# Graph network kernel: filler matmuls placed anew at three places, and one source one-hot per short tile made by ScalarE

## The reference, cut to what matters

```python
msg = x[src] @ W_msg.T + b_msg + edge_embed[type]
messages = segment_sum(msg, dst)                       # one row per node
r, z = sigmoid(...), sigmoid(...)                      # GRU gates from messages and x
n = tanh(i_n + r * h_n)
x1 = layernorm(x + (1 - z) * n + z * x)
h = relu(x1 @ w_self1 + mean_agg(x1, src, dst) @ w_neigh1 + b1)
y = h @ w_self2 + mean_agg(h, src, dst) @ w_neigh2 + b2
out = layernorm(x1 + y)
```

## Time and profile before

| | |
|---|---|
| median of 3 runs | 734.29 us (732.76 to 736.21) |
| the profiled execution | 735.67 us; its span from first to last instruction 733.9 us |
| mean clock granted to TensorE | 0.971 of full |
| TensorE busy | 648.3 us, 88% of the span |
| VectorE busy | 466.9 us, 64% |
| ScalarE busy | 242.2 us, 33% |
| GpSimd busy | 165.0 us, 22% |

### The profile page before, as it was taken

How to read it: one execution, slowest core, us unless ns; L and a number is a source line. 1 busy time by engine, 2 the same in 40 slices (tenths; PEclk the granted TensorE clock), 3 DMA queues, 4 the chain that set the end, 5 groups by cost and what they waited for, 6 DMA issues and landing times.

```text
span 733.9 us, 14577 instructions
## 1 busy us (share of the span) xinstructions
PE 648.3 (88%) x3061; PEld 308.6 (42%) x3061; DVE 466.9 (64%) x1469; ACT 242.2 (33%) x486; POOL 165.0 (22%) x348
## 2 busy tenths in 40 slices
PE   1668889999999999898967999789999999999995
PEld 0222333443433444343323444334555546666663
DVE  6879999999999999999992366641010001144334
ACT  3034553442332255566763245531121122100000
POOL 2432233333223333343430012130111011100000
PEclk9969999999999999999996999989999999999998
DMA  5000000000000000000011011010111011212200
GB/s 161 1 1 0 1 1 0 1 1 1 1 0 1 1 1 1 0 1 1 1 35 51 15 36 51 17 46 15 44 43 43 1 43 41 82 44 61 62 25 16
DMA packets 29441, 17.38 MB, mean 24 GB/s; under 512 B 1841, under 2 KB 28223, under 8 KB 29400
## 3 DMA queue, kind: packets, MB, share of 16 engines
q1 hardware_dynamic: 29400, 16.82, 7.8%
HBM read 10.38 MB, written 6.44 MB: 23 GB/s over the span
## 4 chain that ended last, share of the span: by engine, by line
PE 59%; DVE 22%; issue 9%; DVEq 6%; ACT 2%; POOL 0%; ACTq 0%; POOLq 0%
DVE S L624 12%; PE PS L1267 11%; PE PS L923 11%; PE PS L996 9%; PE PS L880 5%; DVE D L618 4%; PE PS L1178 3%; PE PS L1057 3%; PE PS L1105 2%; DVEq L624 2%; PE PS L1231 2%; PE PS L1094 2%; PE PS L1166 2%; PE PS L1167 1%; PE PS L1030 1%
## 5 line engine op out<-in xcount | busy, mean ns | idle before, releaser
L624 DVE TENSOR_SCALAR S<-iota_h,src_col,src_w 128x440 bf16<-128x440 f16 x749 | 253.2, 399 | 0.2 <-issue 0.2
L923 PE MATMUL PS<-S,D 128*128 128x449 bf16 x780 | 213.1, 363 | 36.8 <-DVE S L624 32.9
L477 POOL COPY S<-T 128x27 bf16 (+1 forms) x262 | 107.6, 412 | 222.2 <-PE PS L923 210.0
L923 PEld LDWEIGHTS PS<-S,D 128*128 128x128 bf16 x780 | 75.3, 97 | 169.2 <-DVE S L624 127.7
L1310 ACT ACTIVATE AT<-digits 128x1152 uint8 (+5 forms) x75 | 77.2, 1031 | 148.6 <-DVE digits L613 148.6
L618 DVE TENSOR_TENSOR D<-iota_t,dst 128x384 bf16<-128x384 f16 x260 | 93.5, 360 | 13.9 <-PE PS L923 13.2
L880 PE MATMUL PS<-AT,xp 128*128 128x512 bf16 x375 | 100.6, 379 | 0.0
L1267 PE MATMUL PS<-xp,AT 128*128 128x384 bf16 (+1 forms) x525 | 85.6, 326 | 0.0
L996 PE MATMUL PS<-AT,x1p 128*128 (+2 forms) x375 | 68.8, 342 | 1.2 <-DVE slot L806 1.2
L1267 PEld LDWEIGHTS PS<-xp,AT 128*128 (+2 forms) x525 | 51.5, 98 | 33.9 <-issue 0.3
L923 PE MATMUL PS<-S,AT 128*128 128x449 bf16 x150 | 35.9, 378 | 19.2 <-DVE S L624 10.5
(11 more groups left out here) (167 smaller groups left out, 664.7 us busy)
## 6 DMA issues: line engine op xcount, KB each, us to landing
slot<-x_rows SPq DMA_DIRECT2D x12, 256.0 KB, 2.9
xstage<-x SPq DMA_DIRECT2D x6, 256.0 KB, 5.5
x_rows<-slot SPq DMA_DIRECT2D x6, 256.0 KB, 2.2
y_rows<-slot SPq DMA_DIRECT2D x6, 256.0 KB, 2.2
res_rows<-slot SPq DMA_DIRECT2D x6, 256.0 KB, 2.2
slot<-res_rows SPq DMA_DIRECT2D x6, 256.0 KB, 2.8
out_rows<-slot SPq DMA_DIRECT2D x6, 256.0 KB, 2.2
slot<-xT SPq DMA_DIRECT2D x3, 256.0 KB, 2.7
```

The lines of the kernel that those rows point to most:

```text
L477: g.tensor_copy(S[:, where:where + V, SPAN:WIDE], T[:, :, ds(c0 + where, V)].rearrange("p k c -> p c k")).then_inc(sem("types_placed"), 1)
L624: v.tensor_scalar(S[:, u, 0:SPAN], iota_h[:, :], src_col[:, ds(c0 + u, 1)], src_w[:, ds(c0 + u, 1)], ALU.is_equal, ALU.mult).then_inc(sem( ...
L923: mm(PS[:, par, 0:WIDE], ring[:, u, :], S[:, u, 0:WIDE], start=opens and u == 0, stop=last).then_inc(sem("tiles_summed" if last else "item ...
```

## The change

Four edits. (1) In each of the tiles 0 to 20 ScalarE makes the sixth source one-hot of the last batch (`border_row`), VectorE leaves it out, and TensorE waits for `S_border_set` ahead of that batch's last matmul. (2) ScalarE does `x_mid` in tile 1 in place of tile 2. (3) The first 27 of the 75 matmuls of column block 5 are taken out of `fills` and stand in counting's tail (`tail_sum`), 18 ahead of the verdict's matmul and 9 behind it; block 5 now comes ahead of block 6, so `late_out` copies block 5 in step 1 and block 6 in step 2 (before: block 6 in step 0 and block 5 in step 3). (4) The rest of the fillers are spread anew over the steps of the opening pass.

```diff
+TAIL_STEPS = 9
@@ edge_rows (VectorE), short tiles
-                    one_hots(t, first + more, par, False, lambda: between(2))
+                    one_hots(t, first + more, par, True, lambda: between(2))
@@ one_pass, count_tile (TensorE)
-                                pe.wait_ge(sem(f"S_last_set{t}"), helped)
+                                pe.wait_ge(sem("S_border_set" if closes else f"S_last_set{t}"), helped)
-                one_pass(first + t + more, first + more, D, None, closes=True, between_halves=lambda: early_piece(t, pieces - 1, pieces))
+                one_pass(first + t + more, first + more, D, None if is_dense(t) else t + 1, closes=True, between_halves=lambda: early_piece(t, pieces - 1, pieces))
@@ behind the last turn_tile (TensorE)
+            def tail_sum(j0, j1):
+
+                pe.wait_ge(sem("digits_stored"), TILES * STORES)
+                for j in range(j0, j1):
+                    for s in range(PARTS):
+                        mm(PS[:, 1, :], xp[:, j, s, :], AT[:, j, (NC - 1) * 512:NC * 512], start=(j == 0 and s == 0), stop=False)
+
+            tail_sum(0, 6)
             pe.wait_ge(sem("verdict_set"), 1)
             mm(PS[0:1, 0, 0:1], ones[:, 0:1], verdict[:, :], start=True, stop=True).then_inc(sem("verdict_sum"), 1)
+            tail_sum(6, TAIL_STEPS)
@@ late_sum (TensorE)
-                if q == NC - 1 and j0 == 0:
+                if q == NC:
                     pe.wait_ge(sem("late_out"), 1)
@@ the opening pass (TensorE)
-            fills = {0: (lambda: late_sum(NC, 0, TILES), lambda: late_sum(NC - 1, 0, 4)),
-                     1: (lambda: late_sum(NC - 1, 4, 9), lambda: late_sum(NC - 1, 9, 13)),
-                     2: (lambda: late_sum(NC - 1, 13, 18), lambda: late_sum(NC - 1, 18, 22)),
-                     3: (lambda: late_sum(NC - 1, 22, TILES), lambda: p2_first(0, 4)),
-                     4: (lambda: p2_first(4, 8), lambda: p2_first(8, 10)),
+            fills = {0: (lambda: late_sum(NC - 1, TAIL_STEPS, 13), lambda: late_sum(NC - 1, 13, 17)),
+                     1: (lambda: late_sum(NC - 1, 17, 21), lambda: late_sum(NC - 1, 21, TILES)),
+                     2: (lambda: None, lambda: late_sum(NC, 0, TILES)),
+                     3: (lambda: None, lambda: p2_first(0, 6)),
+                     4: (lambda: p2_first(6, 8), lambda: p2_first(8, 10)),
                      5: (lambda: p2_first(10, 12), lambda: p2_first(12, 15)),
-                     6: (lambda: p2_first(15, 18), lambda: p2_first(18, 20))}
+                     6: (lambda: p2_first(15, 16), lambda: p2_second(9, 16))}
@@
-                if q == NC:
-                    p2_second(0, 6)
+                if q == NC - 2:
+                    p2_second(0, 2)
+                if q == NC - 1:
+                    p2_second(2, 9)
                 rows_back(q)
-            p2_second(6, 20)
-            p2_first(20, TILES - 1)
+            p2_second(16, 20)
+            p2_first(16, TILES - 1)
             p2_second(20, TILES - 1)
@@ ScalarE
+            def border_row(t):
+
+                first, more = tile_entry(act, t)
+                b = first + more
+                c = first_chunk(b) + (U - 1)
+                near = apart[:, 8:16, :]
+                a.activation(near, iota_h[:, :].rearrange("p (a n) -> p a n", a=8), ACT.Abs, scale=-1.0,
+                             bias=src_col[:, ds(c, 1)]).then_inc(sem("border_apart_set"), 1)
+                act.wait_ge(sem("border_apart_set"), t + 1)
+                act.wait_ge(sem("items_done"), items_until(t, b, 1))
+                a.activation(S[:, U - 1, 0:SPAN].rearrange("p (a n) -> p a n", a=8), near, ACT.Relu,
+                             scale=src_wn[:, ds(b.with_bounds(min_val=0, max_val=BATCHES), 1)],
+                             bias=src_w[:, ds(c, 1)]).then_inc(sem("S_border_set"), 1)
@@
             for t in range(LAG):
                 tile_steps(t, (t - 1) % 2)
-                if t == 2:
+                if t == 1:
                     for c in range(NC + 1):
                         x_mid(c)
+                border_row(t)
@@
                     tile_steps(t + n, n)
+                    border_row(t + n)
@@
-                if q == 0:
-                    late_out(1, NC)
-                if q == 3:
-                    late_out(2, NC - 1)
+                if q == 1:
+                    late_out(1, NC - 1)
+                if q == 2:
+                    late_out(2, NC)
```

## The result

The changed kernel took 724.65 us, the median of four runs (722.12 to 727.31), beside 735.25 us for the kernel before in the same measurement: a ratio of 0.9861, with a 95% interval of 0.9815 to 0.9906. By that ratio it is 10.2 us faster (10.6 by the two medians) where 17.0 were predicted; 724.65 lies above the range that was given. Its profiled execution is the slowest of the four, 727.31 us, with a span of 725.6 us and a mean granted clock of 0.980 (0.971 before).

What follows compares the result with a forecast made beforehand. VectorE was taken to bound counting and TensorE most of the opening pass. Border rows 5.4, tiles 0 and 1 with x_mid 4.0, tail 3.7 and opening pass 3.9 sum to 17.0 off 734.29: 717.3 us, range 712.5 to 723.

Steps and rivals of the forecast that it cites:

- What bounds the kernel: Whole kernel: VectorE, 96% busy, sets counting's pace, so an instruction less saves time; the opening pass is mostly TensorE's.
- Border rows: Borders of tiles 2 to 20: one source one-hot less on VectorE saves 0.30 us a tile, 5.4 us in all.
- border rows buy nothing: Rival at the later tiles' borders: TensorE with its early pieces sets them, 5.4 us lost, 722.7 us; chance 0.08.
- Nothing came late: Rival at 19 borders: ScalarE's row comes late and TensorE waits; 744.0 us at the engines' full difference; chance 0.03.
- Tiles 0 to 3: Start of counting: x_mid in tile 1 and four border rows save 4.6 us, as the account splits the forecast.
- Tail and head: Counting's tail and the opening pass's head: 27 fillers cost nothing and keep the clock up, saving 3.7 us.
- Opening pass: Opening pass behind its head: terms together save 6.4 us, less 2.5 for one clock fall, so 3.9 us.
- The waits: Opening pass, steps 1 and 2: TensorE newly waits for VectorE's last row, adding 3.1 and 2.7 us.
- ScalarE's idle 5 us: Opening pass, step 1: sign that ScalarE stands idle about 5 us before late_out.
- the wait of 1.00: Late opening pass: TensorE's waits of 1.00 and 5.70 us are filled by 6 and 21 matmuls, saving 5.6 us.
- Without a fall of the clock: Opening pass: new waits too short to lower the clock, 6.4 us saved; as a rival 714.8 us, chance 0.28.
- the price of the falls: Opening pass, behind the new waits: one fall of the clock counted at 2.5 us, bounded by 1.7 and 3.7.

Runs made afterwards that it cites:

- e2: The changed kernel with VectorE making all six source one-hots again in tiles 0 to 20, fillings and x_mid's place kept: 724.14 us, ratio 0.9841.
- e3: The changed kernel with ScalarE making the first row of the last half batch instead of its last: 720.35 us, ratio 0.9776.
- e12: The kernel before with only x_mid's copies moved from tile 2 to tile 1: 731.71 us, ratio 0.9940.
- e10: The changed kernel with late copies behind the norm's parts, ScalarE's border row first in its half batch, and border rows only from tile 2: 711.04 us, ratio 0.9659.
- e11: The kernel before with 27 unused matmuls added, 18 ahead of the verdict's matmul and 9 behind it: 733.98 us, ratio 0.9971.
- the repeat: The changed kernel run once more without an edit: median 724.74 us, ratio 0.9852; its profiled execution took 720.27 us.
- e4: The changed kernel with 13 and 11 unused matmuls in TensorE's waits of opening-pass steps 1 and 2: 720.78 us, ratio 0.9795.

## Why the prediction was wrong

**What bounds the kernel.** "So VectorE sets the pace of counting, and an instruction less on it is time less", provided that its replacement is ready. The replacement was ready, and the sentence is right inside a tile and wrong at its border. The waits of the earlier trace rows were short, but there were 27 of them, about one a border, and each says that the chain there ends on TensorE.

**Border rows: the step that failed.** "TensorE's next tile begins behind the last one-hot of the batch, and that is now the fifth." It begins behind the last *matmul* of the batch, which is still the sixth. Priced 0.30 a tile, it is worth 0.12 to 0.14 (the account, e2): from VectorE's last row to the border matmuls it is 0.94 us before and 1.13 after. e3 shows the mechanism from the other side: with the sixth row back on VectorE and the fourth on ScalarE it is 0.91. Of the 6.1 to 6.8 us by which the gain fell short (17.0 less 10.2 or 10.9), 2.8 are here (4.8 less 2.0). The rival "border rows buy nothing" named the right engine, but for another reason, the early pieces. Nothing came late: TensorE waited for ScalarE's row once, at tile 1. The rule of the Trainium skill (ScalarE: Activation LUTs, Rules for kernel authors), that simple functions belong on VectorE, agrees with the trace as to speed (ScalarE's two activations take 0.66 and 0.75 us, VectorE's one instruction 0.30). The row left VectorE without a loss, but also for little.

**Tiles 0 to 3.** Mechanism and rows right: TensorE's border matmuls were forecast for 36.2 and VectorE's one-hots for 37.6; less the 0.81 us of a later start they came at 36.45 and 37.91. TensorE's wait there was put at some 2 us and is 1.20. What was left out is that part of it is given back by tile 4 (in e12 0.76 of 4.76): 3.0 to 3.1 in place of 4.6. That tile 1's own row, queued behind the copies, costs more than it brings was in the working, without its price: 1.3 us (e10).

**Tail and head.** Right: 3.57 against 3.7 in the profiles of the changed kernel; by itself (e11) it moved the end by 2.1.

**Opening pass.** The waits were forecast as 3.1 and 2.7 and are 3.12 and 2.67; ScalarE's idle 5 us is 5.21; the wait of 1.00 is gone, that of 5.70 is 0.80, and the 1.0 ahead of the last block's rows is 0.88. Without a fall of the clock the pass was to gain 6.4 and gained 6.64 in the repeat. The step that was mis-sized is the price of the falls, "2.5: I count one such fall": the profiles show none, one or two falls, a single one at 1.4 to 4.4, and in the median run they cost 4.2 (e4). That is 1.7 of the miss. The rest, about 2 us, is by the account the 1.5 of tiles 0 to 3 and the start, less the 0.5 of the dense tiles, which I had not counted and did not follow up; profiles and medians are mixed in this sum, so it is rough.

## What to carry to other kernels

Price an instruction that is taken off the busiest engine by the chain at the place where the engines meet: what the consumer has still to do behind the last input, and whether a piece that another engine supplies can come first and not last. Ask of every copy that waits for a sum whether it must stand ahead of work that is ready; here its place in ScalarE's queue was worth 8.6 us. Measure a stage by an event on its critical chain, and read a releaser's name as a guess until an edit that moves it has moved the wait.

## What was not expected of the hardware

The same wait in the same program brought the clock down in one execution and not in the next: behind 3.12 us TensorE ran at 1.2 GHz for most of 8 us in one profile and at 2.4 GHz throughout in another, and runs of the changed kernel spread over almost 7 us (720.27 to 727.01), against 1.5 us once the waits were filled. The Trainium skill (TensorE: Matmul & The Clock Gate, What's actually happening) says that the gate watches TensorE's activity on a schedule of its own, which is not aligned with the program. By it such a spread is to be expected. The six profiles fit that (low clock behind step 1's wait in five, behind step 2's in one), but no run here shows the schedule itself.
